# A residual added by an accumulating transfer, one tap moved to ScalarE, and all eight key tiles summed on VectorE

## What is computed

```
x = x + attention(gn(x))       # layer 1
x = x + displace(gn(x))        # layer 2
```

```
scores = var_v @ var_k^T * scale      # variance of q and of k per pixel
out = softmax(scores) @ v ; out = out @ W_proj.T + b_proj
```

## Time and profile before

| | |
|---|---|
| median of three runs | 2126.57 us |
| the profiled execution, launch to end | 2135.85 us |
| its span, first to last instruction | 2134.0 us |
| mean granted clock of TensorE | 0.968 |
| busy: TensorE, VectorE, ScalarE, GpSimd | 94%, 79%, 55%, 11% |
| moved by DMA | 214.35 MB, 100 GB/s on average |
| share of the last-ending chain: TensorE, VectorE, DMA, ScalarE | 75%, 10%, 9%, 3% |

### The profile page before, as it was taken

One profiled execution on the slowest core, in us unless ns is written; L12 is line 12 of the kernel. 1 busy time (PEld: TensorE's weight loads), 2 busy tenths in 40 slices (PEclk: granted clock), 3 DMA queues, 4 the chain that ended last, 5 costly groups with the idle time before them and its releaser, 6 DMA issues.

```text
span 2134.0 us, 33573 instructions
## 1 busy us (share of the span) xinstructions
PE 1996.2 (94%) x12956; PEld 1095.8 (51%) x12956; DVE 1686.3 (79%) x3599; ACT 1180.3 (55%) x1285; POOL 227.6 (11%) x263
## 2 busy tenths in 40 slices
PE   3899999999999999999999999999999999999970
PEld 2656446652565536554375534655366543755330
DVE  7487576998589875998769976798769987699748
ACT  5466734766267643677336762576537674367601
POOL 2000001110011100111002100111001110012001
PEclk7999999999999999999999999999999999999985
DMA  6411302334033431335113350243313351133304
GB/s 229 166 51 61 100 1 79 118 119 153 2 101 134 135 100 34 117 110 179 31 51 130 128 157 5 90 130 120 129 31 112 108 177 43 41 130 130 110 1 177
DMA packets 102976, 214.35 MB, mean 100 GB/s; under 512 B 50080, under 2 KB 50848, under 8 KB 102816
## 3 DMA queue, kind: packets, MB, share of 16 engines
q1 hardware_dynamic: 70848, 95.79, 15.1%
q0 software_dynamic: 25920, 94.38, 12.1%
q10 hardware_dynamic: 6048, 22.02, 3.3%
HBM read 154.08 MB, written 57.74 MB: 99 GB/s over the span
## 4 chain that ended last, share of the span: by engine, by line
PE 75%; DVE 10%; DMA 9%; ACT 3%; issue 2%; SPq 1%; POOL 1%; ACTq 0%; DVEq 0%; POOLq 0%
PE ps L1122 31%; PE ps L1157 25%; PE ps L1174 15%; PE ps L1139 4%; ACT ring L609 2%; DVE bst_x L739 2%; DMA a_sb<-a_rows 2%; DMA cs_rows_y<-mv_y 2%; DVE st L765 1%; DMA dt_sb<-d_sb 1%; DMA bt<-r_rows 1%; DVE d_sb L823 1%; DMA r_rows<-dt_sb 1%; DVE xv L882 1%; DVE xv L880 1%
## 5 line engine op out<-in xcount | busy, mean ns | idle before, releaser
L609 ACT ACTIVATE ring<-a_sb,coef 128x1024 f32<-128x1024 f32 x768 | 813.6, 1137 | 20.6 <-PE ps L1157 10.5
L1122 PE MATMUL ps<-wkv_hi,h_sp 128*128 128x256 f16 x4608 | 777.6, 274 | 15.3 <-DVE h_sp L756 9.9
L1157 PE MATMUL ps<-ring,xv 128*64 128x512 f32 x3072 | 688.9, 597 | 1.6 <-ACT ring L609 1.2
L1122 PE MATMUL ps<-wkv_lo,h_sp 128*128 128x256 f16 x2304 | 630.7, 274 | 0.0
L1122 PEld LDWEIGHTS ps<-wkv_hi,h_sp 128*128 128x128 f16 x4608 | 452.6, 98 | 102.2 <-issue 31.0
L813 DVE TENSOR_TENSOR bt<-bt,ring 128x1024 f32<-128x1024 f32 x416 | 485.2, 1213 | 2.4 <-ACT ring L609 1.8
L1157 PEld LDWEIGHTS ps<-ring,xv 128*64 128x64 f32 x3072 | 208.5, 137 | 418.9 <-issue 394.4
L593 ACT ACTIVATE xv<-ps 128x256 f32<-128x256 f32 x192 | 72.7, 383 | 581.9 <-DVE st L765 581.8
L1174 PE MATMUL ps<-xv,wp_hi 128*128 128x512 f16 x1152 | 356.7, 387 | 0.0
L765 DVE BATCH_NORM_STATS2 st<-ps 128x6 f32<-128x64 f32 x1536 | 218.0, 211 | 119.5 <-PE ps L1122 118.8
L1122 PEld LDWEIGHTS ps<-wkv_lo,h_sp 128*128 128x128 f16 x2304 | 226.2, 98 | 26.9
(11 more groups left out here) (122 smaller groups left out, 1295.2 us busy)
## 6 DMA issues: line engine op xcount, KB each, us to landing
a_sb<-a_rows SPq DMA_DIRECT2D x96, 512.0 KB, 4.8
xv<-in_x POOLq DMA_DIRECT2D x48, 512.0 KB, 3.7
h_sp<-in_x ACTq DMA_DIRECT2D x42, 512.0 KB, 4.7
shift_rows<-bt POOLq DMA_DIRECT2D x42, 512.0 KB, 3.2
out<-xv POOLq DMA_DIRECT2D x42, 512.0 KB, 2.9
bt<-r_rows SPq DMA_DIRECT2D x80, 256.0 KB, 3.9
shift_rows<-ring SPq DMA_DIRECT2D x12, 528.0 KB, 14.1
xv<-in_L_conv_W_qkv SPq DMA_DIRECT2D x4, 1152.0 KB, 9.3
```

Of the source, the lines that this page charges most:

```text
L609: nc.scalar.activation(ring_of(p, s, m), a_sb[:, h % 4, :], ACT.Exp, scale=coef[:, h, m:m + 1]).then_inc(s_exp, 1)
L1122: last = nc.tensor.matmul(ps[:, kv_bank[u % 2], half * 2 * P:(half + 1) * 2 * P], h_sp[:, k, hp, m * P:(m + 1) * P], wkv[wpart][:, k, q * ...
L1157: last = nc.tensor.matmul(ps[s * HD:(s + 1) * HD, o_bank[p % 2] + j, :], v_sb[:, p, m, s * HD:(s + 1) * HD], ring_of(p, s, m)[:, j * HALF: ...
```

## The change

- `MD` becomes (8, 8, 8, 8, 5, 5): in pairs 0 to 3 VectorE adds all eight m, and TensorE does one group of denominators, over `acc`, instead of two. The wait for the bank to be free (s_dsb, s_rlast) moves in front of that group.
- The add of m = 7 is issued on VectorE at the end of m = 6's work, behind `kv_stats(b, nxt + 3)` and ahead of `taps_x`.
- GpSimd writes x1 (layer 1's output, the residual) of tile t to the output right after k_reduce(t), signalled by s_res. Later the displaced tile is added to it in DRAM by an accumulating transfer (`accum_op=ALU.add`) instead of a plain write.
- So x1 may be overwritten: ScalarE computes the middle x tap into x1 (`middle_tap_x`, after the exponentials of m = 5, once the y taps, gn and the residual's write are done, s_tapx), and VectorE's `taps_x` keeps two operations. Image 7's layer 2 keeps the three operations (`taps_x_tail`).

```diff
--- before.py
+++ after.py
@@ -261,6 +261,8 @@
         s_sh_tail = [sem(f"s_sh_tail{i}") for i in range(CT)]
         s_tap = sem("s_tap")
         s_pch = sem("s_pch")
+        s_tapx = sem("s_tapx")
+        s_res = sem("s_res")
         s_fin = sem("s_fin")
         s_out = [sem(f"s_out{t}") for t in range(CT)]
         s_out_last = [sem(f"s_out_last{t}") for t in range(CT)]
@@ -282,7 +284,7 @@
             last(B - 1)
 
 
-        MD = (7, 7, 7, 7, 5, 5)
+        MD = (8, 8, 8, 8, 5, 5)
         ADDS_TO = [0]
         for n in MD:
             ADDS_TO.append(ADDS_TO[-1] + 2 * (n - 1))
@@ -501,6 +503,9 @@
                 for t in range(CT + 1):
                     if t < CT:
                         k_reduce(b + 1, t)
+                        pool.wait_ge(s_x1, (b + 1) * PU)
+                        hold(pool, s_held_pool)
+                        pool.dma_start(out_t[b, :, t, :], x1[:, t, :]).then_inc(s_res, 16)
                         pool.wait_ge(s_gn, b * CT + t + 1)
                         hold(pool, s_held_pool)
                         pool.dma_start(shift_rows[t][:, MARGIN:MARGIN + N], g_t).then_inc(s_gst, 16)
@@ -509,8 +514,9 @@
                         windows(t, g_t, s_sh)
                     if t:
                         pool.wait_ge(s_fin, b * CT + t)
+                        pool.wait_ge(s_res, (b * CT + t) * 16)
                         hold(pool, s_held_pool)
-                        pool.dma_start(out_t[b, :, t - 1, :], x1[:, t - 1, :]).then_inc(s_out[t - 1], 16)
+                        pool.dma_start(out_t[b, :, t - 1, :], x1[:, t - 1, :], accum_op=ALU.add).then_inc(s_out[t - 1], 16)
                         pool.wait_ge(s_out[t - 1], b * 16 + 16)
                         hold(pool, s_held_pool)
                         pool.dma_start(x1[:, t - 1, :], x_t[b + 1, :, t - 1, :]).then_inc(s_x1in[t - 1], 16)
@@ -641,6 +647,13 @@
                     act.wait_ge(s_fin, b * CT + t)
                 nc.scalar.activation(t_t, g_t, ACT.Copy, scale=taps[:, t, 1, 1:2]).then_inc(s_tap, 1)
 
+            def middle_tap_x(b, t):
+
+                act.wait_ge(s_pch, b * 3 * CT + 3 * t + 2)
+                act.wait_ge(s_gn, b * CT + t + 1)
+                act.wait_ge(s_res, (b * CT + t + 1) * 16)
+                nc.scalar.activation(x1[:, t, :], t_t, ACT.Copy, scale=taps[:, t, 0, 1:2]).then_inc(s_tapx, 1)
+
             def phase_a(b, beside=None):
                 for u in range(UA):
                     v_evict(b, u)
@@ -663,6 +676,8 @@
                             if p <= 4:
                                 v_evict(b, nxt)
                                 v_evict(b, nxt + 1)
+                        if m == 5 and later:
+                            middle_tap_x(l1, p)
                         if m == 7:
                             if p:
                                 o_first(b, p - 1)
@@ -851,18 +866,18 @@
                 if t == 0:
                     dve.wait_ge(s_msk, b + 1)
                 elif wait_taps:
-                    dve.wait_ge(s_pch, b * 4 * CT + 4 * (t - 1) + 2)
+                    dve.wait_ge(s_pch, b * 3 * CT + 3 * (t - 1) + 2)
                 nc.vector.scalar_tensor_tensor(dst.rearrange("p (y x) -> p y x", x=W),
                                                x1[:, t, :].rearrange("p (y x) -> p y x", x=W), rb["y"][:, t, 1:2],
                                                mask_y[:, t:t + 1, :].broadcast_to((P, H, W)),
                                                ALU.subtract, ALU.mult).then_inc(s_gn, 1)
 
-            def taps_y(b, t, src, mid):
+            def taps_y(b, t, src, mid, per_tile=3):
 
                 sh = src.rearrange("p (y x) -> p y x", x=W)
                 tp = mid.rearrange("p (y x) -> p y x", x=W)
                 ky = taps[:, t, 1, :]
-                n = b * 4 * CT + 4 * t
+                n = b * 3 * CT + per_tile * t
                 dve.wait_ge(s_tap, b * CT + t + 1)
                 nc.vector.scalar_tensor_tensor(tp[:, 1:H, :], sh[:, 0:H - 1, :], ky[:, 0:1], tp[:, 1:H, :],
                                                ALU.mult, ALU.add).then_inc(s_pch, 1)
@@ -875,7 +890,20 @@
                 tp = mid.rearrange("p (y x) -> p y x", x=W)
                 xt = x1[:, t, :].rearrange("p (y x) -> p y x", x=W)
                 kx = taps[:, t, 0, :]
-                n = b * 4 * CT + 4 * t
+                n = b * 3 * CT + 3 * t
+                dve.wait_ge(s_tapx, b * CT + t + 1)
+                nc.vector.scalar_tensor_tensor(xt[:, :, 1:W], tp[:, :, 0:W - 1], kx[:, 0:1], xt[:, :, 1:W],
+                                               ALU.mult, ALU.add).then_inc(s_pch, 1)
+                dve.wait_ge(s_pch, n + 3)
+                nc.vector.scalar_tensor_tensor(xt[:, :, 0:W - 1], tp[:, :, 1:W], kx[:, 2:3], xt[:, :, 0:W - 1],
+                                               ALU.mult, ALU.add).then_inc(s_fin, 1)
+
+            def taps_x_tail(b, t, mid):
+
+                tp = mid.rearrange("p (y x) -> p y x", x=W)
+                xt = x1[:, t, :].rearrange("p (y x) -> p y x", x=W)
+                kx = taps[:, t, 0, :]
+                n = b * 3 * CT + 4 * t
                 dve.wait_ge(s_pch, n + 2)
                 nc.vector.scalar_tensor_tensor(xt, tp, kx[:, 1:2], xt, ALU.mult, ALU.add).then_inc(s_pch, 1)
                 dve.wait_ge(s_pch, n + 3)
@@ -913,7 +941,8 @@
                         kv_stats(b, nxt + 1)
                         variances(b, 1)
                     for m in range(MT):
-                        add_up(b, p, m, later)
+                        if m < MT - 1:
+                            add_up(b, p, m, later)
                         if m == 3:
                             if 1 <= p <= 4:
                                 kv_stats(b, nxt)
@@ -941,6 +970,7 @@
                             if p <= 3:
                                 k_scales(b, p + 1)
                                 kv_stats(b, nxt + 3)
+                            add_up(b, p, MT - 1, later)
                             if later:
                                 taps_x(l1, p, t_t)
                         if m == 7 and p:
@@ -1093,8 +1123,8 @@
                 for t in range(CT):
                     gn(b, t, tail_g[t], False)
                 for t in range(CT):
-                    taps_y(b, t, tail_g[t], tail_t[t % 2])
-                    taps_x(b, t, tail_t[t % 2])
+                    taps_y(b, t, tail_g[t], tail_t[t % 2], 4)
+                    taps_x_tail(b, t, tail_t[t % 2])
 
             run(dve, first, body, last)
 
@@ -1140,6 +1170,13 @@
                                                 tiles[s][:, j * HALF:(j + 1) * HALF], start=start, stop=stop)
                 return last
 
+            def d_bank_free(b, p, later):
+
+                if p:
+                    pe.wait_ge(s_dsb, b * NR + p)
+                elif later:
+                    pe.wait_ge(s_rlast, b)
+
             def weigh(b, p, m, later):
 
                 if m == 0:
@@ -1160,10 +1197,8 @@
                             ring_of(p, s, m)[:, j * HALF:(j + 1) * HALF],
                             start=(m == 0), stop=(m == MT - 1))
                 if m >= MD[p]:
-                    if m == MD[p] and p:
-                        pe.wait_ge(s_dsb, b * NR + p)
-                    if m == MD[p] and p == 0 and later:
-                        pe.wait_ge(s_rlast, b)
+                    if m == MD[p]:
+                        d_bank_free(b, p, later)
                     last = denominators([ring_of(p, s, m) for s in (0, 1)], m == MD[p], False)
                 last.then_inc(s_pv, 1)
 
@@ -1204,7 +1239,9 @@
                                 pe.wait_ge(s_olo, b * NP + NP - 2)
                             project(b, (m - 3) // 2, range(CT - 2))
                     pe.wait_ge(s_acc, b * NADD + ADDS_TO[p + 1])
-                    denominators([acc_of(p, s) for s in (0, 1)], False, True).then_inc(s_d, 1)
+                    if MD[p] == MT:
+                        d_bank_free(b, p, later)
+                    denominators([acc_of(p, s) for s in (0, 1)], MD[p] == MT, True).then_inc(s_d, 1)
 
             def r_spread(b):
```

## The result

| | before | after |
|---|---|---|
| median (9 runs each) | 2128.89 us | 2109.69 us |
| lowest to highest | 2119.9 to 2139.4 | 2106.77 to 2119.35 |
| the profiled execution, launch to end | 2135.85 us | 2119.35 us |
| its span | 2134.0 us | 2117.3 us |
| mean granted clock of TensorE | 0.968 | 0.973 |

The ratio is 0.9919, with a 95% interval of 0.9893 to 0.9945: the changed kernel takes about 17 us less. The forecast was 4 to 5 us less. The time is nearest to rival A's 2107 us; part of rival B, the clock behind the new wait, came about with it. The profiled execution of after is the slowest of its nine runs, but it stands 16.5 us under the profiled one of before, so the two traces may be set against each other.

The account below looks back on a forecast made before the run. TensorE was taken to bound pairs 0 to 3, latency of transfers and VectorE pairs 4 and 5. -11.8 us in the first and +7.5 in the second gave -4.3 on 2126.6: 2122 us, range 2104 to 2145.

Parts of the forecast that it names:

- rival A: Pairs 4 and 5: residual's write and accumulating transfer are covered, -6.3 us there; 2107 us in all, chance 0.25.
- rival B: End of pair 0: TensorE's clock falls in the new wait, 1.7 to 3.3 us per image; 2139 us, chance 0.13.
- the new wait: End of pair 0: TensorE stands 2.5 us for VectorE's last add in seven images, 0.5 taken for image 0.
- slow clock spared: TensorE's slow clock saved where its wait for the reciprocal goes: some 2 us, counted in rival A only.
- Regimes: TensorE's work counts in pairs 0 to 3; latency of transfers and VectorE in pairs 4 and 5 of images 1 to 6.
- Denominators: Pairs 0 to 3: one group of four matmuls less per pair saves TensorE 0.925 us, at most 29.6 us in all.
- VectorE fits: Pairs 0 to 3: VectorE's loop grows from 29.40 to 30.5 us and stays within TensorE's 31.0.
- The middle tap on ScalarE: Pairs 4 and 5: the 1.14 us tap falls mostly into ScalarE's idle time; 0 to 0.2 us per image, 0.2 taken.
- the chain of pairs 4 and 5: Transfers and taps after pair 3's end: +1.25 us per image, +7.5 us over six images.
- Residual's write: Pair 5's preparation: the added write delays a's rows and the a_sb broadcast; 0 to 3.7 us, 1.4 taken per image.
- Accumulate: Pairs 4 and 5: the accumulating output transfer ahead of d_sb's copies costs 0 to 2.0 us, 0.9 taken on the chain.
- The tap off VectorE: Pair 5: one VectorE tap less on the chain, -1.25 us for images 1 to 6.

Follow-up runs that it names:

- the other trace: The changed kernel, unaltered, run once more beside the follow-up kernels on their chip: ratio 0.9923 (0.9896 to 0.995) to the kernel before.

## Why the prediction was right or wrong

**The time: in the range, but in part by luck.** It lies 3 us above rival A's. A had the chain's sign right (-6.3, measured -8.0), but left out the clock behind the new wait (+6.8) and took 2 us of slow clock spared where the trace has 10; these two errors nearly cancel.

**Regimes: right for pairs 0 to 3,** which are TensorE's. In pairs 4 and 5 the chain ends last in before, but only by 1.9 us per image on average (11.5 us of waits in six). In after it is 0.6 us, close to a balance.

**Denominators: right, 7% too dear.** 0.86 us a group, not 0.925: the chain's 1.85 us for two groups hold an end that is paid once, since one group alone takes 1.00 there in after, and 1.85 - 1.00 = 0.85. 32 groups are 27.5, not 29.6 us. Pairs of 31.06 us against 31.0 forecast.

**VectorE fits: right,** 30.72 of 31.0 us busy against 30.5. The fear that it would hold up pairs 2 and 3 was empty even with the third tap left on it.

**The new wait: right** at 2.50 to 2.52 us against 2.5 in seven images, and 0.50 in image 0. The chain of after shows the cause that was named, statistics and two adds behind each other.

**Rival B: right in part.** The fall was given as a case by itself, seven times at 1.7 to 3.3 us. It comes in four (five in the other trace), at the lower price: +7 us. The sum left it out.

**The middle tap on ScalarE: as said.** In the kernel with no added transfers the copy of d_sb is 0.3 us earlier than in before, so nothing of the tap is seen there.

**The failed step is the chain of pairs 4 and 5,** +1.25 us per image in the sum and -1.2 us in the trace (57.63 to 56.42 at the spread of r; -0.8 in the second trace of after). Its terms:
- *Residual's write*, 1.4 in the sum: 0.5 at the copy of d_sb and at o. a's rows land later behind it, but with them the a_sb broadcast moves away from the write of g, and takes 5.7 us on average instead of 7.4 (8 to 9 was forecast). I charged the new transfer where it stands and left the old collision where it stood.
- *Accumulate*, 0.9 in the sum: its landing grows by 2.0 us, the upper end, and o comes 1.25 us later. This term was about right on the chain; the spread sees 0.5 of it.
- *The tap off VectorE*, -1.25: the chain of after has one tap less than that of before between o and the reciprocal. No run takes this tap alone.
- *Not in the sum*: in the kernel without added transfers o is 1.8 us earlier than in before, though pair 5's tap has not come by then. 0.3 of it is there at the copy of d_sb, and 0.8 comes between the copy and the reciprocal, where dt_sb is spread (5.2 us from its first issue to its last landing, against 6.0). What makes it so is open.

0.5 + 1.25 - 1.25 - 1.8 = -1.3, against -1.2 in the trace.

**The slow clock spared: left out of the sum, 2 us in rival A, 10 in the trace.** The prediction used to price the new wait and not the old ones. Of five images with a fall after the spread of r in before, one is left in after, two in its second trace.

The miss by terms, measured less forecast: denominators +2.1, clock behind the new wait +6.8, chain -8.0 - 7.5 = -15.5, clock spared -10.2, start, image 5 and pair 5 +3.8: -13.0 in all, which takes the -4.3 to -17.3 (-17.1 above; the rest is rounding). The chain and the clock behind it are the miss.

## What to carry to other kernels

When work is moved from the bound engine to a nearly full one, look for the stage in which the receiver starts late, and leave that stage as it is: with the tap moved, seven tiles in pair 0 and eight in pairs 1 to 3 give a ratio of 0.9864, eight in all four 0.992, seven in all four 0.9932. A wait of the bound engine has two prices, its length and the slow clock behind it; count both for the waits that go as for those that come. A transfer added in front of a chain also moves those behind it, so read which collisions it undoes before charging its bytes.

## What the runs showed of the hardware

- An accumulating transfer of 512 KB from SBUF to DRAM takes GpSimd 0.87 to 1.01 us to issue (plain: 0.53 to 0.58), and lands 2.0 to 2.5 us later than the plain one (median of 42 from issue 5.4 us in after, 2.9 with the plain write).
- The granted clock after a wait of TensorE between full matmuls: waits of 2.50 to 2.52 us were followed by a fall in 28 of 42 cases (six traces), 1.7 us lost each; waits of 1.45 to 1.47 us in none of nine. Ahead of the spread of r, whose matmuls have one row, waits of 0.9 to 1.7 us were followed by a fall in 9 of 19 cases and those of 1.75 to 4.2 us in all nine (all twelve traces). A short one, 1.00 us in before, and its stretch, 8.5 us at a mean of 0.80, or 1.7 us lost:

```profile
1532.88 1.09 PE L1215 MATMUL ps<-d_sb,ones 1*64 1x512 f32 x8 [1.00 <-DVE d_sb L823]
```
```profile
1531.50:1540.00 8.50, 7.50 (x31) 2.70 (x30) 6.54 (x13) 2.09 (x2) 0.00 (x0) 0.80 0.05 3
```

- A small write among bulk transfers has no fixed landing: the 8 KB of a's rows took 4.3 us on average in before, 5.3 in the kernel without added transfers and 6.2 with the residual's write ahead of them.
